# Two-layer attention kernel on TensorE: the order of scores and value blocks in each slot, and what fills the first pass

## Chip, cores and metric

One core of one Trainium2 chip. The metric is the device time of one execution in microseconds (us); runs are compared by their medians.

## What is computed

Two transformer layers on 1024 tokens of 256 features, in float32. The change touches the two 16-head attentions (head size 16): layer 0 reads 4096 given keys and values, layer 1 the 1024 tokens themselves.

```
mod = (_silu(c) @ wmod).reshape(c.shape[0], 6, 1, -1)      # sa, ca, ga, sb, cb, gb, for both layers
h = _layernorm(x, axis=-1) * (1 + ca) + sa
scores = jnp.einsum('bqhd,khd->bhqk', Q, K) * SCALE
attn = jax.nn.softmax(scores, axis=-1)
out = jnp.einsum('bhqk,khd->bqhd', attn, V).reshape(B, QL, HIDDEN)
x = x + ga * (out @ Wo.T)
```

A routed feed-forward follows the first attention, and the normalisation, a causal 16-head attention with 128 features per head and an expert layer follow the second; none of these is edited.

## The kernel before

Class `Attention` runs both attentions; `nkt` is the number of 128-key tiles (32 in the first, called long here; 8 in the second, called short). The work is cut into 32 units: one head and one half (512) of the queries, `u` in the code. The softmax needs the maximum of every query first, so the scores are made twice.

The **first pass** makes scores with queries as output rows. One chunk is 128 queries by 1024 keys: two matmuls (`first_half`, L646) into two of the PSUM banks 0 to 3, one for each strip of the array's rows (rows 0 to 47 hold one part of the keys, rows 64 to 111 the other). VectorE reduces the chunk to its maxima (L786 long, L782 short) and so frees the two banks; two chunks fit at a time. GpSimd splits the maxima into three bf16 parts (`split_max`, L572 to L578), TensorE turns them (`turn_maxima`, L668, L673), and ScalarE writes the row of queries with their maxima (`put_row`, L835).

The **second pass** makes scores with keys as output rows: one matmul for 128 keys (`second_chunk`, L705), on the strip of even or of odd `j`, into one of the banks 4 to 6. ScalarE takes the exponential (L878). Four exponentials make a group, and the **values** of a group (`pv_half`, L686) are four float32 matmuls, side by side in four 32-column parts of the array, into bank 7; a half has 256 query columns, and each float32 matmul appears as two passes in the trace. When a unit's last group is done, the sums in bank 7 are copied out by ScalarE in the long attention (L843) and by VectorE in the short one (L800), and the next unit's first values wait for that copy (`o_full`).

TensorE's order is written by hand in `slot(u, g)`: four second-pass chunks, two first-pass chunks that run `ahead` of them (22 chunks in the long attention, 10 in the short one), and two value halves of the group before. A unit has eight slots in the long attention and two in the short one. Ahead of the first slot, a loop makes the chunks that run ahead. In the long attention it also makes the adaLN modulation (`Front.later_products`): column products (L1051, output 128x1) and row products (L1058, output 128x256). `keep_busy` (L1133) issues bf16 matmuls of 128x128 whose result nobody reads. In the short attention the products of the values (L1246) stand between the first chunks.

Of the kernel before, what the change touches and what calls it, by code (L numbers as in the profile page):

```python
# [18 lines left out]
DC = D // P  # L19
H = 16  # L20
HD = 16
QH = 512
# [294 lines left out]
class Attention:  # L317


    def __init__(self, nc, ctx, psum, ident, ident_bf, tag, nkt, nb, o_dram, k_dram=None, v_dram=None, v_sb=None):  # L320
# [14 lines left out]
        self.pair_last = self.groups >= 8  # L335
        self.sums_by_act = self.groups >= 8
# [63 lines left out]
    def filling(self, j):  # L400
        return j + (j >= self.turn_at)
# [73 lines left out]
    def run(self, block, load_q, load_kr, q_loads, merge, projection, stats, front=None, weights=None):  # L475
# [5 lines left out]
        ahead = steps + self.shift  # L481
# [75 lines left out]
        def _(pool):  # L557
# [71 lines left out]
        def _(pe):  # L629
# [46 lines left out]
            def pv_half(u, n, half):  # L676

                b, cols = (u // 2) % nb, slice(half * (QH // 2), (half + 1) * (QH // 2))
                pe.wait_ge(self.exp_done, u * nkt + group * (n + 1))
                if n == 0 and half == 0:  # L680
                    if u > 0:
                        pe.wait_ge(self.o_full, u)
                    pe.wait_ge(self.v_ready, u // 2 + 1)
                for j in range(group * n, group * (n + 1)):
                    g, block_at = j % 4, (j % 2) * (nkt // 2) + j // 2
                    mm = pe.matmul(psum[32 * g:32 * g + 32, 7, cols], self.v_ext[:, b, block_at, :], self.probs[:, j % self.pring, cols],  # L686
                                   start=(j < 4 and half == 0), stop=(j >= nkt - 4 and half == 1))
                if half == 1:
                    mm.then_inc(self.pv_done, 1)

            def values_behind(u, g, half):

                if g > 0:
                    pv_half(u, g - 1, half)
                elif u > 0:
                    pv_half(u - 1, groups - 1, half)
# [11 lines left out]
            def second_pair(two):  # L708
                if two < self.chunks:
                    first_wait(two)  # L710
                    first_half(two, 0)
                    first_half(two, 1).then_inc(self.s1_full, 1)

            def slot(u, g):

                j = group * g
                one = u * steps + 2 * g + ahead
                two = one + 1
                steps_here = self.steps_after(u, g)
                second_wait(u, j)  # L720
                second_chunk(u, j)
                if one < self.chunks:
                    first_wait(one)
                    first_half(one, 1)
                    first_half(one, 0).then_inc(self.s1_full, 1)
                second_wait(u, j + 1)
                second_chunk(u, j + 1)
                values_behind(u, g, 0)
                if not self.pair_last:
                    second_pair(two)  # L730
# [6 lines left out]
                second_wait(u, j + 3)  # L737
                second_chunk(u, j + 3)
                if self.pair_last:
                    second_pair(two)  # L740
                values_behind(u, g, 1)
# [9 lines left out]
            for n in range(ahead):  # L751
                first_wait(n)
                first_half(n, 0)
                first_half(n, 1).then_inc(self.s1_full, 1)
                if n + values_ahead < projection.tiles:
                    projection.value_products(pe, n + values_ahead)
                if front is not None:
                    front.later_products(pe, n)
            projection.banks_free(pe)
            if front is not None:  # L760
                front.banks_free(pe)
            keep_busy(pe, psum, self.ident_bf, 8)
            turn_maxima(0)
            keep_busy(pe, psum, self.ident_bf, 8)
            for u in range(us):
                for g in range(groups):
                    slot(u, g)
            for half in range(2):
                pv_half(us - 1, groups - 1, half)
# [5 lines left out]
        def _(dve):  # L775
# [31 lines left out]
            for u in range(us):  # L807
                for s in range(steps):
                    if s == 2 and u > 0 and not self.sums_by_act:
# [12 lines left out]
            if not self.sums_by_act:  # L822
                take_sums(us - 1)
# [7 lines left out]
        def _(act):  # L831
# [36 lines left out]
            for u in range(us):  # L868
                for j in range(nkt):
# [3 lines left out]
                    if j == group and u > 0 and self.sums_by_act:  # L873
                        take_sums(u - 1)
# [5 lines left out]
            if self.sums_by_act:  # L880
                take_sums(us - 1)
# [6 lines left out]
class Front:  # L888
# [10 lines left out]
    def __init__(self, room, psum, space, ident, ident_bf, mod_col, mod_row, gates, x, h_t, wq):  # L899
# [27 lines left out]
        groups = [("col", i, c) for i in range(2, len(self.COLS)) for c in range(DC)] + [("row", i, 0) for i in range(len(self.ROWS))]  # L927
        self.groups = sorted(groups, key=lambda g: (self.COLS if g[0] == "col" else self.ROWS)[g[1]][0])
        self.first_chunk = 2

# [134 lines left out]
    def later_products(self, pe, n):  # L1065


        at = n - self.first_chunk
        if not 0 <= at < len(self.groups):
            return  # L1070
        kind, i, c = self.groups[at]
        if at == 0:
            pe.wait_ge(self.wide_ready, 2 * DC)
# [6 lines left out]
    def stay_busy(self, pe):  # L1080


        keep_busy(pe, self.psum, self.ones_bf, 75, 3)
# [1445 lines left out]
```

## Time and profile before

| | before |
|---|---|
| median of 3 runs | 1801.67 us (1797.59 to 1803.48) |
| profiled execution, own time | 1802.71 us |
| profiled execution, span of its instructions | 1800.9 us |
| TensorE, busy share of the span | 96% |
| VectorE | 77% |
| ScalarE | 64% |
| GpSimd | 29% |
| TensorE's mean granted clock, of full speed | 0.976 |

The long attention lies between about 27 and 747 us of the span, the short one between about 804 and 1047 us. Busy shares are averages over stages with different limits, and a busy TensorE at half its clock does half the work; so the stage, its clock and its waits have to be read together.

### The profile page before, as it was taken

Reading aid. Unit: us, or ns where it says so; the run is one execution under the profiler, and the core shown is the slowest. Engines: PE = TensorE matmul, PEld = TensorE weight load, DVE = VectorE, ACT = ScalarE, POOL = GpSimd, SP = SyncE. Lnnn points to the kernel's source line nnn. Section 1 sums busy time; section 2 is a strip of 40 time slices with the busy share of each in tenths; the row PEclk is TensorE's granted clock in tenths of the full one; section 3 lists DMA queues with packets and bytes.
Section 4 is the critical chain, followed back from the end, with each engine's and each line's share of the span. In section 5 each row is a group of like instructions: output and inputs, shape, how many; then the busy total and the mean of one; then the engine's idle time right before and its main releaser. Section 6 shows DMA issues by size and latency. Waiting matters only on the chain. (4 is left out here: it accounts for less than half of the span.)

```text
span 1800.9 us, 34561 instructions
## 1 busy us (share of the span) xinstructions
PE 1720.8 (96%) x13014; PEld 1057.5 (59%) x13017; DVE 1392.3 (77%) x1927; ACT 1147.9 (64%) x2277; POOL 518.5 (29%) x535
## 2 busy tenths in 40 slices
PE   9999999999999999889999989999999999889998
PEld 6433333333333333564444468888888888768886
DVE  5699999999999997367999667777777777746665
ACT  2488888888888888554777635455545554533333
POOL 7247334333344522011334311111211120142221
PEclk8699999999999999989999999999999999989999
DMA  7122232223322300103537210000000000033332
GB/s 174 24 45 59 55 54 50 45 52 70 78 46 57 70 26 11 36 18 61 129 92 167 74 32 16 9 23 15 23 9 23 15 12 1 19 84 109 115 102 77
DMA packets 50309, 97.94 MB, mean 54 GB/s; under 512 B 11481, under 2 KB 21817, under 8 KB 48651
## 3 DMA queue, kind: packets, MB, share of 16 engines
q1 hardware_dynamic: 49899, 95.78, 22.5%
q8 instruction: 82, 1.34, 0.3%
q10 hardware_dynamic: 288, 0.49, 0.2%
q14 instruction: 40, 0.33, 0.1%
HBM read 64.58 MB, written 15.92 MB: 45 GB/s over the span
## 5 line engine op out<-in xcount | busy, mean ns | idle before, releaser
L878 ACT ACTIVATE a_probs<-psum 128x512 f32<-128x512 f32 x1280 | 690.4, 598 | 111.5 <-PE psum L705 81.9
L786 DVE TENSOR_REDUCE a_max_part<-psum 128x1 f32<-128x1024 f32 x512 | 622.0, 1223 | 50.6 <-PE psum L646 48.8
L686 PE MATMUL psum<-a_probs,a_v_ext 128*32 128x256 f32 x5120 | 411.7, 393 | 14.8 <-ACT a_probs L878 7.5
L705 PE MATMUL psum<-a_q_max,a_k_rows 51*128 51x512 f32 x1280 | 399.5, 469 | 0.4 <-ACT a_q_max L835 0.2
L646 PE MATMUL psum<-a_k_rows,a_q_rows 48*128 48x512 f32 x1280 | 367.8, 441 | 4.7 <-DVE a_max_part L786 3.0
L705 PEld LDWEIGHTS psum<-a_q_max,a_k_rows 51*128 51x128 f32 x1280 | 162.4, 185 | 236.7 <-ACT a_probs L878 181.8
L686 PEld LDWEIGHTS psum<-a_probs,a_v_ext 128*32 128x32 f32 x5120 | 103.1, 108 | 238.6 <-ACT a_probs L878 200.5
L646 PEld LDWEIGHTS psum<-a_k_rows,a_q_rows 48*128 48x128 f32 x1280 | 154.9, 189 | 39.1 <-issue 26.2
L782 DVE TENSOR_REDUCE a_neg_max<-psum 128x1 f32<-128x1024 f32 x128 | 153.3, 1222 | 11.0 <-PE psum L646 10.9
L2182 PE MATMUL psum<-high_t_parts,high_gu 128*128 128x512 f32 x600 | 149.0, 398 | 9.1 <-POOL high_gu L2300 7.6
L429 POOL TENSOR_TENSOR a_k_rows<-a_k_in,a_k_rows 16x2048 fp32r<-16x2048 f32 x32 | 146.0, 4562 | 2.5
L572 POOL TENSOR_TENSOR a_max_bf<-a_neg_max,a_zeros 128x8 bf16<-128x8 f32 x64 | 14.7, 229 | 456.0 <-issue 396.5
L2182 PEld LDWEIGHTS psum<-high_t_parts,high_gu 128*128 128x128 f32 x600 | 114.0, 191 | 36.6 <-POOL high_gu L2300 8.2
L1746 PE MATMUL psum<-wide_k_t,wide_q_t 128*128 128x512 f32 (+3 forms) x576 | 130.6, 353 | 1.5 <-DVE wide_k_t L1944 1.5
L1746 PE MATMUL psum<-wide_p_t,wide_v 128*128 128x512 f32 (+3 forms) x576 | 109.5, 343 | 5.1 <-DVE x L1955 5.1
L1746 PEld LDWEIGHTS psum<-wide_p_t,wide_v 128*128 128x128 f32 x576 | 97.6, 188 | 22.3 <-issue 6.3
L1887 ACT ACTIVATE wide_probs<-psum,wide_neg_max 128x128 f32<-128x128 f32 (+7 forms) x128 | 96.5, 754 | 21.6 <-DVE wide_neg_max L1977 21.6
L1966 DVE TENSOR_TENSOR wide_p_t<-psum,wide_p_t 128x512 fp32r<-128x512 f32 (+1 forms) x192 | 100.0, 548 | 12.4 <-ACT wide_p_t L1872 12.4
L1746 PE MATMUL psum<-wide_t_parts,wide_wqk 128*128 128x512 f32 x384 | 102.2, 401 | 6.1 <-DVE wide_v L1944 3.9
L1872 ACT ACTIVATE wide_p_t<-psum 128x512 fp32r<-128x512 f32 (+1 forms) x192 | 87.1, 492 | 28.0 <-PE psum L1787 27.9
L1746 PEld LDWEIGHTS psum<-wide_k_t,wide_q_t 128*128 128x128 f32 x576 | 94.0, 189 | 12.6 <-issue 1.9
L1977 DVE TENSOR_REDUCE wide_neg_max<-psum 128x1 f32<-128x128 f32 (+7 forms) x128 | 97.0, 758 | 4.4
(263 smaller groups left out, 2146.3 us busy)
## 6 DMA issues: line engine op xcount, KB each, us to landing
o<-a_o_out SPq DMA_DIRECT2D x56, 256.0 KB, 2.2
a_k_in<-in_k SPq DMA_DIRECT2D x96, 128.0 KB, 4.5
a_q_rows<-q_high SPq DMA_DIRECT2D x124, 64.0 KB, 2.4
gu_in<-in_w_gu SPq DMA_DIRECT2D x25, 256.0 KB, 2.8
high_cw<-cw SPq DMA_DIRECT2D x22, 256.0 KB, 4.0
a_v_in<-in_v SPq DMA_DIRECT2D x16, 256.0 KB, 5.8
a_o<-o SPq DMA_DIRECT2D x8, 512.0 KB, 4.8
wide_qk_in<-in_wqk SPq DMA_DIRECT2D x16, 256.0 KB, 2.7
```

Of the source, the lines that this page charges most:

```text
L429: pool.tensor_tensor(self.k_rows[low, b, :], self.k_in[low, :], self.k_rows[low, b, :], ALU.subtract).then_inc(self.k_split, 1)
L646: return pe.matmul(psum[:, 2 * (n % 2) + s, :], q_rows[rows, b, q0:q0 + P], k_rows[rows, b, k0:k0 + 512], start=True, stop=True)
L686: mm = pe.matmul(psum[32 * g:32 * g + 32, 7, cols], self.v_ext[:, b, block_at, :], self.probs[:, j % self.pring, cols], start=(j < 4 and h ...
L705: pe.matmul(psum[:, self.bank_of(self.filling(j)), :], k_rows[rows, b, k0:k0 + P], self.q_max[rows, u % 2, :], start=True, stop=True).then ...
L782: dve.tensor_reduce(self.neg_max[:, u % 2, c:c + 1], psum[:, 2 * (n % 2):2 * (n % 2) + 2, :], AX.XY, ALU.max, negate=True).then_inc(self.s ...
L786: dve.tensor_reduce(self.max_part[:, u % 2, c // self.nch, c % self.nch:c % self.nch + 1], psum[:, 2 * (n % 2):2 * (n % 2) + 2, :], AX.XY, ...
L878: act.activation(self.probs[:, p % self.pring, :], psum[:, self.bank_of(self.filling(j)), :], ACT.Exp).then_inc(self.exp_done, 1)
L1746: mm = pe.matmul(out, left(a), right(b), start=(first and n == 0), stop=(last and n == len(PARTS) - 1))
L1887: act.activation(probs[:, i % 2, 0:(i + 1) * P], bank_pair(i)[:, 0:(i + 1) * P], ACT.Exp, bias=neg_max[:, i:i + 1], accum_out=den[:, h % 2 ...
L1966: dve.tensor_tensor(turned_of(i, bank, 1), turned_from(i, bank), turned_of(i, bank, 0), ALU.subtract).then_inc(pt_lo, 1)
L1977: dve.tensor_reduce(neg_max[:, i:i + 1], bank_pair(i)[:, 0:(i + 1) * P], AX.X, ALU.max, negate=True).then_inc(max_ready, 1)
L2182: mm = pe.matmul(psum[:, 2 * (k % 2) + i, :], gu[:, par, a, at:at + P], t_parts[:, b, c, half * 512:(half + 1) * 512], start=(c == 0 and n ...
```

## The change

Four edits. (1) The modulation products are ordered anew: two row products stand ahead of the first chunk, the rest alternate, and `keep_busy` matmuls fill the wait between chunks: three ahead of a chunk with a column product, none ahead of one with a row product, six ahead of one with none. `turn_maxima(0)` moves from behind the loop into it, behind chunk `steps + 2`, with the wait for the free banks; on GpSimd `split_max(0)` moves ahead of the second `copy_v`. (2) In the short attention (`slot_short`) the second first-pass chunk moves up, and the two value halves become one block of 512 columns at the slot's end. (3) The unit without values behind it (`u = 0`, `g = 0`) gets `keep_busy` in their place. (4) In the long attention's second slot (`g == 1`) the third score stands ahead of the first value half.

```diff
                 for h in range(1, self.early):
                     self.split_keys(pool, h)
+                split_max(0)
+                for h in range(1, self.early):
                     self.copy_v(pool, h)
-                split_max(0)
...
+            def values_whole(u, n):
+                values_wait(u, n)
+                values_part(u, n, slice(0, QH), True, True)
...
+            def slot_long(u, g):
+
+                j, ready = group * g, u * steps + 2 * g + ahead
+                behind = (u, g - 1) if g > 0 else (u - 1, groups - 1)
+                steps_here = self.steps_after(u, g)
+                second(u, j)
+                first_pair(ready, (1, 0))
+                second(u, j + 1)
+                if g == 1:
+                    second(u, j + 2)
+                if behind[0] >= 0:
+                    values_half(*behind, 0)
+                else:
+                    keep_busy(pe, psum, self.ident_bf, 8)
+                if g != 1:
+                    second(u, j + 2)
...
+                second(u, j + 3)
+                first_pair(ready + 1, (0, 1))
+                if behind[0] >= 0:
+                    values_half(*behind, 1)
...
+            def slot_short(u, g):
...
+                second(u, j)
+                first_pair(ready, (1, 0))
+                second(u, j + 1)
                 if j + 2 == self.turn_at and u + 1 < us:
                     turn_maxima(u + 1)
+                first_pair(ready + 1, (0, 1))
                 second_wait(u, j + 2)
                 second_chunk(u, j + 2)
...
+                second(u, j + 3)
+                if behind[0] >= 0:
+                    values_whole(*behind)
+                else:
+                    keep_busy(pe, psum, self.ident_bf, 16)
...
             projection.products(pe, front)
             if front is not None:
-                front.stay_busy(pe)
+                projection.banks_free(pe)
+                front.first_products(pe)
...
             for n in range(ahead):
+                t = n + values_ahead
                 first_wait(n)
+                if n >= 2:
+                    filling = front.filling(n) if front is not None else 0 if t < projection.tiles else 6
+                    keep_busy(pe, psum, self.ident_bf, filling, 2 * (n % 2))
                 first_half(n, 0)
...
+                if n == steps + 2:
+                    if front is not None:
+                        front.banks_free(pe)
+                    else:
+                        projection.banks_free(pe)
+                    turn_maxima(0)
...
+        self.groups = [("row", 0, 0), ("row", 1, 0), ("col", 2, 0), ("col", 2, 1), ("col", 3, 0), ("row", 2, 0), ("col", 3, 1),
+                       ("row", 3, 0), ("col", 4, 0), ("row", 4, 0), ("col", 4, 1), ("row", 5, 0), ("col", 5, 0), ("col", 5, 1)]
...
-        keep_busy(pe, self.psum, self.ones_bf, 75, 3)
+    def first_products(self, pe):
+
+
+        keep_busy(pe, self.psum, self.ones_bf, 45, 3)
+        pe.wait_ge(self.wide_ready, 2 * DC)
+        for at in range(self.at_once):
+            self.group_product(pe, at)
```

TensorE's rows at the start of the long attention's first pass, before (`a_c_wide` with `a_o` is a row product, `a_c_silu` a column product; in the changed file the same statements have other line numbers: L1182 is `keep_busy`, L1089 and L1096 the products, L710 `second_chunk`, L689 the values):

```order
L1236 MATMUL psum<-h_t,wq 128x512 x8
L1133 MATMUL psum<-a_ones_bf 128x128 x75
L646 MATMUL psum<-a_k_rows,a_q_rows 128x512 x6
L1051 MATMUL psum<-a_c_silu,a_o 128x1 x2
L646 MATMUL psum<-a_k_rows,a_q_rows 128x512 x2
```

and now:

```order
L1285 MATMUL psum<-h_t,wq 128x512 x8
L1182 MATMUL psum<-a_ones_bf 128x128 x45
L1096 MATMUL psum<-a_o,a_c_wide 128x256 x4
L646 MATMUL psum<-a_k_rows,a_q_rows 128x512 x4
L1182 MATMUL psum<-ident_bf 128x128 x3
L646 MATMUL psum<-a_k_rows,a_q_rows 128x512 x2
L1089 MATMUL psum<-a_c_silu,a_o 128x1 x2
```

Two row products have come ahead of chunk 0, and three fillings ahead of chunk 2.

The long attention's second slot on TensorE, before (`a0_o_full` is the copy of the sums):

```order
L705 MATMUL psum<-a_q_max,a_k_rows 128x512 [waits a0_exp_done]
L646 MATMUL psum<-a_k_rows,a_q_rows 128x512 [waits a0_s1_free]
L646 MATMUL psum<-a_k_rows,a_q_rows 128x512
L705 MATMUL psum<-a_q_max,a_k_rows 128x512 [waits a0_exp_done]
L686 MATMUL psum<-a_probs,a_v_ext 32x256 [waits a0_v_ready,a0_o_full,a0_exp_done]
L686 MATMUL psum<-a_probs,a_v_ext 32x256 x3
L705 MATMUL psum<-a_q_max,a_k_rows 128x512 [waits a0_exp_done] x2
```

and now:

```order
L710 MATMUL psum<-a_q_max,a_k_rows 128x512 [waits a0_exp_done]
L646 MATMUL psum<-a_k_rows,a_q_rows 128x512 [waits a0_s1_free]
L646 MATMUL psum<-a_k_rows,a_q_rows 128x512
L710 MATMUL psum<-a_q_max,a_k_rows 128x512 [waits a0_exp_done] x2
L689 MATMUL psum<-a_probs,a_v_ext 32x256 [waits a0_v_ready,a0_o_full,a0_exp_done]
L689 MATMUL psum<-a_probs,a_v_ext 32x256 x3
L710 MATMUL psum<-a_q_max,a_k_rows 128x512 [waits a0_exp_done]
L646 MATMUL psum<-a_k_rows,a_q_rows 128x512 [waits a0_s1_free]
```

One score has moved from behind the value half that waits for `a0_o_full` to ahead of it, and the score that stood beside it stays behind.

A unit of the short attention on TensorE, before, from its turned maxima to the next unit:

```order
L668 MATMUL psum<-a_q_rows,a_ident_r 115x512
L673 MATMUL psum<-ident_bf,a_max_bf 115x128 x4
L705 MATMUL psum<-a_q_max,a_k_rows 128x512 x2
L686 MATMUL psum<-a_probs,a_v_ext 32x256 x4
L705 MATMUL psum<-a_q_max,a_k_rows 128x512
L646 MATMUL psum<-a_k_rows,a_q_rows 128x512 x2
L705 MATMUL psum<-a_q_max,a_k_rows 128x512
L686 MATMUL psum<-a_probs,a_v_ext 32x256 x4
L646 MATMUL psum<-a_k_rows,a_q_rows 128x512 x2
L705 MATMUL psum<-a_q_max,a_k_rows 128x512 x2
```

and now:

```order
L668 MATMUL psum<-a_q_rows,a_ident_r 115x512 [waits a1_exp_done]
L673 MATMUL psum<-ident_bf,a_max_bf 115x128 [waits a1_max_ready]
L673 MATMUL psum<-ident_bf,a_max_bf 115x128 x3
L646 MATMUL psum<-a_k_rows,a_q_rows 128x512 [waits a1_s1_free]
L646 MATMUL psum<-a_k_rows,a_q_rows 128x512
L710 MATMUL psum<-a_q_max,a_k_rows 128x512 [waits a1_exp_done] x2
L689 MATMUL psum<-a_probs,a_v_ext 32x512 [waits a1_exp_done]
L689 MATMUL psum<-a_probs,a_v_ext 32x512 x3
L710 MATMUL psum<-a_q_max,a_k_rows 128x512 [waits a1_row_ready]
L646 MATMUL psum<-a_k_rows,a_q_rows 128x512 [waits a1_q_loaded3,a1_s1_free]
```

Four value halves of a unit have become two blocks, each at the end of its slot, and the first-pass chunk that stood behind the turned maxima's half now follows the turned maxima.

## Rows read from the trace of the kernel before

**Rows 1.** Windows: us, busy of TensorE, its weight loads, VectorE, ScalarE, GpSimd; granted clock; DMA.
```profile
30.40:40.60 10.20, 10.20 (x30) 6.37 (x30) 6.98 (x6) 0.00 (x0) 5.87 (x2) 0.50 0.81 129
...
86.60:107.30 20.70, 20.45 (x201) 7.81 (x197) 19.56 (x17) 18.29 (x35) 12.54 (x7) 1.00 0.37 64
```

**Rows 2.** Timeline of TensorE, first pass and first slots, long attention: start, us, group [idle before].
```profile
23.02 4.35 PE L1133 MATMUL psum<-a_ones_bf 128*128 128x128 bf16 x75
29.14 0.51 PE L646 MATMUL psum<-a_k_rows,a_q_rows 48*128 48x512 f32 x2 [1.09 <-DVE a_max_part L786]
...
35.93 2.07 PE L1058 MATMUL psum<-a_o,a_c_wide 128*128 128x256 f32 x4
...
41.63 0.50 PE L646 MATMUL psum<-a_k_rows,a_q_rows 48*128 48x512 f32 x2
...
42.60 0.49 PE L646 MATMUL psum<-a_k_rows,a_q_rows 48*128 48x512 f32 x2
...
64.90 0.79 PE L705 MATMUL psum<-a_q_max,a_k_rows 51*128 51x512 f32 x1
...
79.47 0.50 PE L705 MATMUL psum<-a_q_max,a_k_rows 51*128 51x512 f32 x1
...
81.93 0.49 PE L705 MATMUL psum<-a_q_max,a_k_rows 51*128 51x512 f32 x1
```

**Rows 3.** Timeline of VectorE and GpSimd, the same stretch.
```profile
23.70 1.29 DVE L1283 SCALAR_TENSOR_TENSOR q_low<-psum,q_high 128x512 fp32r<-128x512 f32 x2 [2.59 <-ACT q_high L1268]
27.86 4.62 DVE L786 TENSOR_REDUCE a_max_part<-psum 128x1 f32<-128x1024 f32 x4 [2.88 <-PE psum L646]
38.33 9.09 POOL L429 TENSOR_TENSOR a_k_rows<-a_k_in,a_k_rows 16x2048 fp32r<-16x2048 f32 x2
```

**Rows 4.** Timeline of TensorE, value products between chunks, short attention.
```profile
821.98 1.13 PE L1246 MATMUL psum<-wqkv,h_t 128*128 128x256 f32 x4
```

**Rows 5.** Timeline of TensorE and ScalarE, a second slot of the long attention.
```profile
113.10 0.73 PE L646 MATMUL psum<-a_k_rows,a_q_rows 48*128 48x512 f32 x2
114.08 0.64 PE L686 MATMUL psum<-a_probs,a_v_ext 128*32 128x256 f32 x8 [0.25 <-issue]
113.38 0.60 ACT L843 ACTIVATE a_o_out<-psum 128x512 f32<-128x512 f32 x1
```

**Rows 6.** TensorE's waits, 78 to 706 us: us in total, times, longest.
```profile
PE psum L686 <- issue: 7.2, 29, 0.2
```

**Rows 7.** Timeline of TensorE, one unit of the short attention.
```profile
847.83 0.51 PE L646 MATMUL psum<-a_k_rows,a_q_rows 48*128 48x512 f32 x2
848.26 0.49 PE L668 MATMUL psum<-a_q_rows,a_ident_r 112*115 112x512 f32 x1
...
849.34 0.64 PE L686 MATMUL psum<-a_probs,a_v_ext 128*32 128x256 f32 x8
849.91 0.49 PE L705 MATMUL psum<-a_q_max,a_k_rows 51*128 51x512 f32 x1
...
850.84 0.64 PE L686 MATMUL psum<-a_probs,a_v_ext 128*32 128x256 f32 x8 [0.19 <-ACT a_probs L878]
...
854.31 0.48 PE L668 MATMUL psum<-a_q_rows,a_ident_r 112*115 112x512 f32 x1
```

**Rows 8.** Timeline of VectorE and ScalarE, the same unit; below, the copy's group in the page's manner.
```profile
847.35 2.36 DVE L782 TENSOR_REDUCE a_neg_max<-psum 128x1 f32<-128x1024 f32 x2 [0.22 <-PE psum L646]
846.12 2.08 ACT L878 ACTIVATE a_probs<-psum 128x512 f32<-128x512 f32 x4 [0.60 <-PE psum L705]
L800 DVE COPY a_o_out<-psum 128x512 f32<-128x512 f32 x32 | 22.1, 691 | 10.2 <-PE psum L686 10.2
```

**Rows 9.** Timeline of TensorE, short attention: its first second-pass scores and one of its last units.
```profile
835.09 0.79 PE L705 MATMUL psum<-a_q_max,a_k_rows 51*128 51x512 f32 x1
...
842.21 0.49 PE L668 MATMUL psum<-a_q_rows,a_ident_r 112*115 112x512 f32 x1
...
1023.32 0.64 PE L686 MATMUL psum<-a_probs,a_v_ext 128*32 128x256 f32 x8 [0.99 <-ACT a_probs L878]
```

More of the change, by code:

```diff
@@ L334, in __init__ @@
         self.early = 2
-        self.pair_last = self.groups >= 8
-        self.sums_by_act = self.groups >= 8
+        self.long = self.groups >= 8
         self.room = room = Room(nc, ctx, tag, CLEARED)
@@ L683, in pv_half, with values_part @@
                     pe.wait_ge(self.v_ready, u // 2 + 1)
+            def values_part(u, n, cols, first, last):
+                b = (u // 2) % nb
                 for j in range(group * n, group * (n + 1)):
@@ L686, in pv_half, with values_half @@
                     mm = pe.matmul(psum[32 * g:32 * g + 32, 7, cols], self.v_ext[:, b, block_at, :], self.probs[:, j % self.pring, cols],
-                                   start=(j < 4 and half == 0), stop=(j >= nkt - 4 and half == 1))
-                if half == 1:
+                                   start=(j < 4 and first), stop=(j >= nkt - 4 and last))
+                if last:
                     mm.then_inc(self.pv_done, 1)
[L691 to L696, printed above, removed]
+            def values_whole(u, n):
+                values_wait(u, n)
+                values_part(u, n, slice(0, QH), True, True)
+            def values_half(u, n, half):
+                if half == 0:
+                    values_wait(u, n)
+                values_part(u, n, slice(half * (QH // 2), (half + 1) * (QH // 2)), half == 0, half == 1)
             def second_wait(u, j):
@@ L706, in second_chunk, with first_pair @@
                           self.q_max[rows, u % 2, :], start=True, stop=True).then_inc(self.s2_full, 1)
[L708 to L719, printed above, removed]
+            def first_pair(n, order):
+                if n < self.chunks:
+                    first_wait(n)
+                    first_half(n, order[0])
+                    first_half(n, order[1]).then_inc(self.s1_full, 1)
@@ L720, in slot, with second @@
+            def second(u, j):
+                if j == self.turn_at and u + 1 < us:
+                    turn_maxima(u + 1)
                 second_wait(u, j)
                 second_chunk(u, j)
[L722 to L730, printed above, removed]
+            def slot_long(u, g):
[13 more added lines that the diff above has]
+                    second(u, j + 2)
+                for k in steps_here[:1]:
+                    merge.product(pe, k)
+                second(u, j + 3)
[3 more added lines that the diff above has]
+                else:
+                    keep_busy(pe, psum, self.ident_bf, 8)
+                for k in steps_here[1:]:
+                    merge.product(pe, k)
@@ L731, in slot @@
+            def slot_short(u, g):
+                j, ready = group * g, u * steps + 2 * g + ahead
+                behind = (u, g - 1) if g > 0 else (u - 1, groups - 1)
+                steps_here = self.steps_after(u, g)
+                second(u, j)
+                first_pair(ready, (1, 0))
+                second(u, j + 1)
                 if j + 2 == self.turn_at and u + 1 < us:
                     turn_maxima(u + 1)
+                first_pair(ready + 1, (0, 1))
                 second_wait(u, j + 2)
@@ L751, in _ @@
             for n in range(ahead):
+                t = n + values_ahead
                 first_wait(n)
+                if n >= 2:
+                    filling = front.filling(n) if front is not None else 0 if t < projection.tiles else 6
+                    keep_busy(pe, psum, self.ident_bf, filling, 2 * (n % 2))
                 first_half(n, 0)
                 first_half(n, 1).then_inc(self.s1_full, 1)
-                if n + values_ahead < projection.tiles:
-                    projection.value_products(pe, n + values_ahead)
+                if t < projection.tiles:
+                    projection.value_products(pe, t)
                 if front is not None:
                     front.later_products(pe, n)
[L759 to L764, printed above, removed]
+                if n == steps + 2:
+                    if front is not None:
+                        front.banks_free(pe)
+                    else:
+                        projection.banks_free(pe)
+                    turn_maxima(0)
             for u in range(us):
                 for g in range(groups):
-                    slot(u, g)
-            for half in range(2):
-                pv_half(us - 1, groups - 1, half)
+                    if self.long:
+                        slot_long(u, g)
+                    else:
+                        slot_short(u, g)
+            values_whole(us - 1, groups - 1)
             for k in range(in_slots, merge.STEPS):
@@ L808, in _ @@
                 for s in range(steps):
-                    if s == 2 and u > 0 and not self.sums_by_act:
+                    if s == 2 and u > 0 and not self.long:
                         take_sums(u - 1)
@@ L821, in _ @@
                     merge.reciprocals(dve, 1)
-            if not self.sums_by_act:
+            if not self.long:
                 take_sums(us - 1)
@@ L872, in _ @@
                         put_row(u + 1)
-                    if j == group and u > 0 and self.sums_by_act:
+                    if j == group and u > 0 and self.long:
                         take_sums(u - 1)
@@ L1078, in later_products, with filling @@
             mm.then_inc(self.later_full, 1)
-    def stay_busy(self, pe):
-        keep_busy(pe, self.psum, self.ones_bf, 75, 3)
+    def first_products(self, pe):
[3 more added lines that the diff above has]
+            self.group_product(pe, at)
+    def later_products(self, pe, n):
+        at = n - self.first_chunk + self.at_once
+        if n >= self.first_chunk and at < len(self.groups):
+            self.group_product(pe, at)
+    def filling(self, n):
+        at = n - self.first_chunk + self.at_once
+        if at >= len(self.groups):
+            return 6
+        return 3 if self.groups[at][0] == "col" else 0
     def banks_free(self, pe):
```

22 lines of the change are left out of this document (5 added, 17 removed).

## The prediction

> **What bounds the kernel now.** I read the page's clock and busy rows first, then windows of each stage, then the timeline of TensorE there, then what its waits end on. A steady slot of the long attention is TensorE's: in 86.6 to 107.3 us it is busy 20.45 of 20.70 us at full clock, with VectorE close behind at 19.56 [rows 1]. The slot lasts 2.46 (79.47 to 81.93) [rows 2]. A value half holds the array 0.57 (849.34 to 849.91, the same instructions in the short attention) [rows 7], so the four score steps of a slot take (2.46 - 2 x 0.57) / 4 = 0.33 each. Two places are worse than that. In the long attention's first pass TensorE is busy all of 30.4 to 40.6, yet at a granted clock of 0.50, the lower of its two levels, 1.2 GHz [rows 1]; the first four slots, 64.90 to 79.47, take 14.57 instead of 9.84 [rows 2]. And a unit of the short attention takes 6.05 (848.26 to 854.31) [rows 7], where its work, below, is shorter.
>
> **Edit 1 and 3, the long front.** The fillings now stand behind q_low, whose two operations end at 23.70 + 1.29 = 24.99 [rows 3]. A filling is 4.35 / 75 = 0.058 [rows 2], so 45 end at 27.6. No row shows a row product at full clock; half of the 2.07 that one took at the lower clock is 1.03 [rows 2], and four passes of the same size took 1.13 at full [rows 4]. I take 1.06. Two put chunk 0 at 29.72, and VectorE's first reduction, half a microsecond behind its pair, at 30.26: 2.4 later than the 27.86 of before [rows 3]. From there VectorE's pace is 4.62 / 4 = 1.155 [rows 3], and chunk 2 waits for the first reduction's end, 31.42. A chunk with a column product takes TensorE 0.97 at full clock (41.63 to 42.60) [rows 2], with three fillings 1.14: VectorE's pace stands. A chunk with a row product takes 0.43 (a pair, 847.83 to 848.26 [rows 7]) + 1.06 = 1.49. Chunks 2 to 13 have eight of the one and four of the other, 8 x 1.155 + 4 x 1.49 = 15.2, to 46.6. Seven paces on, chunk 21 starts at 54.7; with its pair, and 0.3 for the part of the turned maxima that VectorE's lead doesn't cover, the first score stands at 55.4 instead of 64.90 [rows 2]. That is **-9.5**, if the clock stays at full.
>
> The fillings of the last chunks hide in VectorE's pace: six are 0.35, beside 0.43 of a pair. The moved turn hangs on GpSimd, whose key split ends at 38.33 + 9.09 = 47.42 [rows 3]; chunk 15, the last that unit 0 needs, is reduced about 49 to 50, so the key split ends first, and with `split_max(0)` ahead of the second `copy_v` the turn finds its maxima about when TensorE gets there. If it waited for `copy_v` again, that would be about 1 us. The first four slots at full clock, one with 16 x 0.058 of fillings in place of its values, are 2.2 + 3 x 2.46 = 9.6 instead of 14.57: **-5.0**. Bounds for both: 0, and -16 if the turn costs nothing. What is late next is VectorE, which then paces the front alone.
>
> The clock is the open term. Before, it fell behind a stretch whose longest idle was 1.09 us [rows 2], rose by itself, and fell once more behind pairs and column products without a wait (from 41.63 [rows 2] on; at 64.90 a score takes 0.79, at 79.47 0.50). Now chunks 2 to 4 are again pairs and column products, with three fillings each, but 45 fillings and two row products stand ahead, and row products alternate behind. In the Trainium skill, TensorE: Matmul & The Clock Gate, the section on why this matters for your kernels puts a lost clock down to long idle gaps between bursts. By that rule the front would not have fallen before; the trace has it fall behind 1.09 us and behind no idle, so the measurement decides, and the rule alone would give the 14.5 for certain.
>
> **Edit 4, the long second slot.** The first value half waits there for ScalarE's copy of the sums (113.38 + 0.60 = 113.98) and starts at 114.08 [rows 5]; the trace counts 29 such waits, 7.2 us together, 0.25 each [rows 6]. A slot has two score steps ahead of the half, 0.66, and the half starts 0.98 behind the slot (113.10 to 114.08) [rows 5]: 0.32 are lost, the slot is 2.78. Now the third score fills that wait. But scores run two abreast, one on each strip, and this one stood beside the fourth on the other strip. Alone it holds the array a step of 0.33, and the fourth one then pairs with half a first-pass chunk and leaves the other half alone: five steps in place of four, 2.46 + 0.33 = 2.79. The wait goes and the time stays: 31 x 0.01, **+0.3**; ends -8 (both wait and step gone: 31 x 0.25) and +3 (a step 0.1 dearer). I take the middle because the steps on one strip are counted, not guessed. The Trainium skill, TensorE: Matmul & The Clock Gate, Part 3 (the mechanism), says that a weight load passes a running matmul only if the row groups differ; for a score alone on its strip that would make the step dearer, towards the +3, and no run here shows it.
>
> **Edit 2, the short loop.** A pass of 256 columns alone takes 1.13 / 4 = 0.28 [rows 4], some 2 x 0.107 (256 columns at 2.4 GHz) and a rest. A half block's eight passes take 0.57, so its four column parts run abreast: two passes one behind the other, 2 x 0.21 = 0.43 that grows with the columns, and 0.14 that I take not to. A whole block is then 0.86 + 0.14 = 1.00, against 1.14 for two halves: 2 x 0.14 a unit. The other bound is 1.14, nothing saved. The wait of 0.19 at 850.84 [rows 7] goes, since the block stands at the slot's end. Two pairs that stood alone at 0.43 [rows 7] stand beside scores at 0.33 now: 0.2. So TensorE's work falls from 6.05 to 5.38. VectorE's own is four reductions of 2.36 / 2 = 1.18, less their overlap 1.15, and a copy of 0.69: 5.3 [rows 8]. A new wait: ScalarE needs 2.08 / 4 = 0.52 an exponential [rows 8], scores now stand close together ahead of the block, and the last of a group waits for a bank: some 0.15. I take 5.5, a gain of 0.55; ends 0.28 (only the columns' part) and 0.75 (down to VectorE). Behind 842.21 there are 28 units at this pace: 28 x 0.55 = **-15.4** (-8 to -21). What is late next is VectorE. The front of this attention: from 835.09 to 842.21 the first unit takes 7.12 [rows 9], 1.07 over the loop's pace, because it starts behind fillings and at the lower clock; a full-clock start and the earlier turn give **-2.4** (0 to -4). In the tail two waits of 1.0 (one at 1023.32 [rows 9], one alike 8.6 later) lose their cause: **-2.0** (0 to -2).
>
> **The sum.** -9.5 - 5.0 + 0.3 - 15.4 - 2.4 - 2.0 = -34.0, made against the profiled execution of 1802.71 us: 1768.7. The median is 1.0 under that execution, so I forecast **1768**.
>
> **Rivals.** *The clock falls again in chunks 2 to 5* (34%). For it: pairs and column products stood there when it fell before. Against: the fillings. At the lower clock the slots took 14.57 / 9.84 = 1.48 times as long; 1.48 to 2 times the 15.2 of chunks 2 to 13 is 7 to 15 more, and the first score stands at 63 to 70 against 64.90. The front then gives nothing, -3 to +5: 1782, 1778 to 1788. *The short loop stays at its pace* (8%): a new wait takes the whole 0.55, for instance the turn behind `put_row`, or ScalarE. 1783; with the clock's fall as well (5%) 1797. *Slower: a 512-column value block does not run abreast as the halves do* (6%). Eight passes at 0.28 would be 2.2 where a half takes 0.57, so the halves run abreast; but no row shows a block of 512. Two abreast, its eight passes of 0.43 to 0.53 would take 1.7 to 2.1. From 1.28 on the loop gains nothing; from 1.71 on (28 x 2 x 0.43 = 24) it eats the front's 19 and 5 more, and at 1.8 to 2.1 the kernel takes 1812 to 1829. *The change does less than it says*: edit 4 does, by my own count; it is in the sum.
>
> **How the numbers follow.** The forecast has 47%: 1768, its own ends 1762 and 1778. The clock's fall and the unchanged short loop stand at 1782 and 1783. The range 1762 to 1788 takes these in and leaves out the two together, the slower case, and what lies under 1762. A measurement of this kernel can tell about 0.3%, 5.4 us, from no change. Under 1796: 47 + 34 + 8 = 89%. Within: 5%. Over: 6%.
>
> **What would show it.** Right: a granted clock of 1.00 from 30 to 60 us, the first score near 55, slots of 2.46 from there; no wait at the first value half of second slots, but slots of 2.79 still; units of 5.5 in the short attention with a block near 1.0. Wrong: a score of 0.79 in the first slots (clock), a second slot near 2.5 (edit 4 priced too low), a value block over 1.28, or a new wait of 0.5 on `a_exp_done` or `a_row_ready` in each short unit.

## The result, and the profile after

Twenty executions of the changed kernel have a median of 1796.46 us (1775.25 to 1810.96), twenty of the kernel before 1801.21. The ratio is 0.9939, with an interval of 0.9913 to 0.9964: by the ratio about 11 us faster, where 1768 was forecast and 1762 to 1788 was the range. The ratios, here and below, leave out executions more than 1.5% above the fastest of their kernel, here eight of the changed kernel, seven of them with the lowest clocks, and one of before; the two medians over all twenty lie only 4.7 apart.

The twenty don't lie around their median. Three are at 1775 to 1781, nine at 1791 to 1798, one at 1802, seven at 1808 to 1811, and TensorE's mean granted clock goes with them: 0.984 to 0.989 in the first three, 0.971 to 0.977 in the nine, 0.963 to 0.967 in the seven. The profiled execution is one of the long ones, 1808.55, span 1806.7, clock 0.965. Windows of its long attention (us; busy of TensorE, weight loads, VectorE, ScalarE, GpSimd; clock; DMA) show where:

```profile
24.50:32.70 8.20, 7.11 (x73) 5.49 (x73) 3.28 (x3) 0.59 (x2) 5.09 (x3) 1.00 0.65 101
32.90:68.70 35.80, 35.80 (x150) 23.17 (x150) 22.05 (x20) 2.50 (x9) 14.79 (x8) 0.50 0.37 62
68.90:118.00 49.10, 49.10 (x271) 17.91 (x268) 27.67 (x24) 25.18 (x46) 14.79 (x8) 0.50 0.13 25
118.20:138.90 20.70, 20.70 (x201) 7.98 (x197) 19.15 (x18) 17.74 (x34) 0.89 (x4) 1.00 0.14 31
```

One stretch at the lower clock reaches from 32.8 to 118.1, over the first pass and some eleven slots behind it (a unit has eight), TensorE busy throughout. Before, two stretches at the lower clock ended at 40.6 and 78.2. The timeline of TensorE at its start, the first score, and a slot's length at half clock, from behind the first value half of one slot to the same place in the next:

```profile
28.88 0.73 PE L646 MATMUL psum<-a_k_rows,a_q_rows 48*128 48x512 f32 x4
30.70 0.34 PE L1182 MATMUL psum<-ident_bf 128*128 128x128 bf16 x3 [1.09 <-DVE a_max_part L823]
30.97 0.50 PE L646 MATMUL psum<-a_k_rows,a_q_rows 48*128 48x512 f32 x2
31.40 0.60 PE L1089 MATMUL psum<-a_c_silu,a_o 128*128 128x1 f32 x4
...
33.64 0.79 PE L646 MATMUL psum<-a_k_rows,a_q_rows 48*128 48x512 f32 x2
...
68.79 0.62 PE L710 MATMUL psum<-a_q_max,a_k_rows 51*128 51x512 f32 x1
...
75.65 0.79 PE L710 MATMUL psum<-a_q_max,a_k_rows 51*128 51x512 f32 x1
...
79.97 0.79 PE L710 MATMUL psum<-a_q_max,a_k_rows 51*128 51x512 f32 x2
```

The wait of 1.09 for chunk 0's reduction is still there [rows 2], chunks 2 to 4 are pairs and column products with three fillings, and the pair of chunk 4, at 33.64, takes 0.79 instead of 0.50. The first score is at 68.79 (64.90 before), the last score of the long attention at 763.29 (743.06): 20.2 lost where 14.2 gained was forecast. Of that, 3.9 is the first pass and 16.3 the slots. A slot at half clock takes 4.32 (75.65 to 79.97), one at full clock 2.46 [rows 2]: 1.76 times as long, not twice. Behind the first score, 49 us ran at half clock where before 13.3 did; the 36 more cost 36 x (1 - 1/1.76) = 15.5 by these rows, an estimate, which is nearly all of the 16.3.

In the second slots the 29 waits [rows 6] are gone: the waits of TensorE between 120 and 725 us are empty. A unit still takes 20.64 us (20.65 before). A unit of the short attention takes 5.70 instead of 6.05 [rows 7]. TensorE in one, then ScalarE and a weight load of TensorE (PEld):

```profile
873.13 0.50 PE L710 MATMUL psum<-a_q_max,a_k_rows 51*128 51x512 f32 x1
...
873.93 0.88 PE L710 MATMUL psum<-a_q_max,a_k_rows 51*128 51x512 f32 x2
874.74 1.06 PE L689 MATMUL psum<-a_probs,a_v_ext 128*32 128x512 f32 x8
875.73 0.49 PE L710 MATMUL psum<-a_q_max,a_k_rows 51*128 51x512 f32 x1
...
876.40 0.49 PE L668 MATMUL psum<-a_q_rows,a_ident_r 112*115 112x512 f32 x1
...
877.84 1.06 PE L689 MATMUL psum<-a_probs,a_v_ext 128*32 128x512 f32 x8
878.83 0.49 PE L710 MATMUL psum<-a_q_max,a_k_rows 51*128 51x512 f32 x1
```

```profile
873.66 2.06 ACT L915 ACTIVATE a_probs<-psum 128x512 f32<-128x512 f32 x4 [0.46 <-PE psum L710]
874.31 0.18 PEld L710 LDWEIGHTS psum<-a_q_max,a_k_rows 51*128 51x128 f32 x1 [0.42 <-ACT a_probs L915]
```

A block holds the array 0.99 (874.74 to 875.73). The third and fourth score of a second slot stand 0.81 ahead of it, where a step of two is 0.33: that is a new wait, 0.42 of the fourth's weight load (874.31) for an exponential. From the first short chunk to the first score the two traces give 15.03 and 13.30, from there to the turn of unit 29 170.54 and 160.48, from there to the last score 27.90 and 26.66. The short attention gained 1.73 + 10.06 + 1.24 = 13.0, of 19.8 forecast.

### The profile page after: what moved, and what is told of

The parts are those of the page before. It is cut to its first block and busy times, and to the rows that moved or that the text cites. A ratio compares the mean times of both kernels' runs of the same rounds, so it can differ in the third digit from the quotient of the medians.

```text
span 1806.7 us, 33654 instructions
## 1 busy us (share of the span) xinstructions
PE 1742.8 (96%) x12560; PEld 1066.0 (59%) x12563; DVE 1391.1 (77%) x1927; ACT 1147.2 (63%) x2277; POOL 518.5 (29%) x535
## 5 line engine op out<-in xcount | busy, mean ns | idle before, releaser
L710 PE MATMUL psum<-a_q_max,a_k_rows 51*128 51x512 f32 x1280 | 424.8, 472 | 0.8 <-ACT a_probs L915 0.7
L689 PE MATMUL psum<-a_probs,a_v_ext 128*32 128x256 f32 (+1 forms) x4600 | 403.9, 423 | 0.4
L646 PE MATMUL psum<-a_k_rows,a_q_rows 48*128 48x512 f32 x1280 | 377.4, 446 | 0.0
L710 PEld LDWEIGHTS psum<-a_q_max,a_k_rows 51*128 51x128 f32 x1280 | 175.9, 188 | 281.8 <-ACT a_probs L915 223.2
L689 PEld LDWEIGHTS psum<-a_probs,a_v_ext 128*32 128x32 f32 x4600 | 92.1, 109 | 203.2 <-issue 133.7
L646 PEld LDWEIGHTS psum<-a_k_rows,a_q_rows 48*128 48x128 f32 x1280 | 160.8, 193 | 10.1 <-issue 5.1
```

Source lines behind the costliest of these rows:

```text
L646: return pe.matmul(psum[:, 2 * (n % 2) + s, :], q_rows[rows, b, q0:q0 + P], k_rows[rows, b, k0:k0 + 512], start=True, stop=True)
L710: pe.matmul(psum[:, self.bank_of(self.filling(j)), :], k_rows[rows, b, k0:k0 + P], self.q_max[rows, u % 2, :], start=True, stop=True).then ...
```

## Which part loses the clock

**The old first pass under the other edits.** The long attention's first pass is put back, and with it the place of `split_max` on GpSimd and the long first slot without fillings (edit 3); the short attention and the long second slot stay changed.

```diff
-                projection.banks_free(pe)
-                front.first_products(pe)
+                front.stay_busy(pe)
...
-                    filling = front.filling(n) if front is not None else 0 if t < projection.tiles else 6
+                    filling = 0 if front is not None or t < projection.tiles else 6
...
+            if front is not None:
+                projection.banks_free(pe)
+                front.banks_free(pe)
+                keep_busy(pe, psum, self.ident_bf, 8)
+                turn_maxima(0)
+                keep_busy(pe, psum, self.ident_bf, 8)
```

> The changed kernel with the long attention's first pass as it was before (75 fillings, products in the old order, no fillings between chunks, the turn behind the loop); the short attention and the long second slot stay changed. Theory F (the new first pass loses TensorE's clock, and the short attention's gain of 13.0, read from the two traces as 1.7 + 10.75 + 0.55, stands in every run): 13 us under before, ratio 0.9928 within 0.0015, and the executions lie as close together as those of before; the clock is back at 1.00 by about 80 us. Rival S (the lone third score of the long second slot keeps the clock down, whatever the first pass does): the executions still scatter by 30 us and the clock comes back later than 100 us in most of them; the ratio is 0.994 or more.

Measured: 1788.90 (1782.78 to 1803.99, 11 executions) against 1805.12, ratio 0.9904 (0.9874 to 0.9935). The 13 us of theory F, 0.9928, lie inside. So undoing the new first pass makes the kernel no slower; whether it makes it faster isn't shown, since the interval overlaps that of the change (0.9913 to 0.9964). Its other half was wrong: the clock is not back by 80 in every execution. In the profiled one, at 1803.99, it came back for 6.6 us and fell again:

```profile
31.20:51.50 20.30, 20.30 (x60) 12.84 (x58) 12.90 (x11) 0.00 (x0) 13.88 (x4) 0.50 0.54 89
51.70:58.30 6.60, 4.71 (x20) 2.37 (x20) 5.79 (x6) 1.90 (x8) 0.90 (x4) 1.00 0.39 60
58.50:123.20 64.70, 64.20 (x350) 24.05 (x350) 37.38 (x34) 31.99 (x59) 15.70 (x12) 0.50 0.13 21
```

**The third score alone**, added to the kernel before.

```diff
+                early = self.pair_last and g == 1
+                if early:
+                    third(u, j + 2)
                 values_behind(u, g, 0)
```

> The kernel before with one edit alone: in the long attention's second slot the third score stands ahead of the first value half. Theory F: no difference, ratio 1.000 within 0.002; a unit of the long attention stays at 20.64 to 20.66 us, the 29 waits of 0.25 are gone. Rival S: the clock stays at half past 100 us in many executions, 5 to 20 us slower. A third reading (the step on one strip costs nothing after all): 7 us faster, a unit of 20.4.

Measured: 1806.34 (12 executions, 1800.11 to 1840.53), ratio 1.0031 (0.9998 to 1.0065), just outside the 0.002 of theory F. No gain: a unit is 20.64, and the waits are gone. Mean clocks were 0.971 over these twelve and 0.975 over the 22 of before; whether the move delays the clock's return by a little is left open.

**The first pass filled.** The row products stand behind chunks 0 and 1, where they cover the wait of 1.09, and thin chunks (a pair with a column product or with nothing behind it) get more fillings.

```diff
-        self.first_chunk = 2
-        self.at_once = 2
+        self.first_chunk = 0
+        self.at_once = 0
...
-            return 6
-        return 3 if self.groups[at][0] == "col" else 0
+            return 8
+        if self.groups[at][0] == "row":
+            return 0
+        return 10 if n in (2, 3, 4, 12, 13) else 3
```

> The changed kernel, but the two row products stand behind chunks 0 and 1 instead of ahead of chunk 0, where they cover TensorE's wait for chunk 0's reduction, and there are ten fillings instead of three ahead of chunks 2, 3, 4, 12 and 13, eight instead of six ahead of 14 to 21. Theory F: the granted clock is 1.00 from 24 us into the slots, the first score stands near 55, the first slots take 2.46; all executions lie between 1770 and 1780, ratio 0.984 within 0.003. If the idle time and the thin products are not what loses the clock: it falls as in the changed kernel, with executions from 1775 to 1810, ratio 0.99 or more.

Measured: 1776.03, all six executions between 1773.92 and 1779.10, mean clock 0.988 to 0.991, ratio 0.9854 (0.9819 to 0.9889). Its windows:

```profile
24.50:32.70 8.20, 6.88 (x72) 5.37 (x72) 3.89 (x5) 1.91 (x3) 4.48 (x3) 1.00 0.86 124
32.90:57.90 25.00, 23.96 (x201) 16.83 (x202) 22.05 (x20) 2.50 (x9) 14.82 (x8) 1.00 0.48 85
58.00:68.20 10.20, 10.20 (x98) 4.40 (x95) 10.06 (x10) 8.23 (x16) 0.00 (x0) 1.00 0.01 2
```

The clock holds in the profiled execution. The first score stands at 57.97, with chunk 0 at 28.43, so it comes 3 later than the 55 expected. The ratio's interval lies below 1 and below that of the change.

**Each half of that alone.** First, only the two row products behind chunks 0 and 1, with the change's own three and six fillings:

```diff
-        self.first_chunk = 2
-        self.at_once = 2
+        self.first_chunk = 0
+        self.at_once = 0
```

> Of the filled front one half alone: the two row products stand behind chunks 0 and 1 (they cover TensorE's wait for chunk 0's reduction), the fillings are the changed kernel's three and six. If the idle 1.09 us is what loses the clock: it holds, executions between 1770 and 1778, a shade under the filled front since five chunks carry seven fillings less, 0.4 each. If the thin products (a pair and a column product a chunk) lose it: it falls between 31 and 36 us and the executions scatter from 1775 to 1810.

Measured: 1781.70 over six executions, against 1796.49 for before at that time. Three lie at 1770 to 1774 (clock 0.991), three at 1790, 1800 and 1806. The profiled one fell:

```profile
24.50:33.80 9.30, 9.22 (x77) 6.70 (x75) 6.09 (x6) 0.00 (x0) 3.63 (x3) 1.00 0.65 113
34.00:85.00 51.00, 51.00 (x243) 27.82 (x241) 30.86 (x27) 12.29 (x27) 14.77 (x8) 0.50 0.19 37
```

TensorE was busy 9.22 of the 9.30 us ahead of the fall. So the clock fell behind three chunks with column products (from 29.6 on) with next to nothing idle. The rule of the Trainium skill that the prediction weighed (TensorE: Matmul & The Clock Gate, why this matters for your kernels), by which long idle gaps lose the clock, doesn't cover this fall. Second, only the fillings, with the row products ahead of chunk 0 and the wait in place:

```diff
-        return 3 if self.groups[at][0] == "col" else 0
+        return 10 if n in (2, 3, 4, 12, 13) else 3
```

> The other half alone: ten fillings ahead of chunks 2, 3, 4, 12 and 13 and eight ahead of 14 to 21, but the two row products ahead of chunk 0 as in the changed kernel, so that the wait of 1.09 us stays. If the idle time loses the clock: it falls near 33 us, executions from 1780 to 1810. If the thin products do: it holds, executions between 1774 and 1781.

Measured: 1776.77 over seven executions, ratio 0.9898 (0.9863 to 0.9934): five at 1772 to 1779, two at 1784 and 1790 with clocks of 0.985 and 0.982. In the profiled one the wait of 1.09 ends at 29.91 and the clock held at 1.00:

```profile
28.09 0.73 PE L646 MATMUL psum<-a_k_rows,a_q_rows 48*128 48x512 f32 x4
29.91 0.73 PE L1184 MATMUL psum<-ident_bf 128*128 128x128 bf16 x10 [1.09 <-DVE a_max_part L823]
...
56.56 0.39 PE L710 MATMUL psum<-a_q_max,a_k_rows 51*128 51x512 f32 x1
```

So neither half alone is the whole cause: by the mean clock each by itself lets most or half of the executions hold, where the change held in two of twenty at 0.988 or more. The small counts don't rank the halves. What remains open is why one execution of a kernel keeps the clock and the next doesn't, and whether the fillings hold it by their own work or by spacing the column products out: no run has a pause of the same length in their place.

**Fewer fillings**, seven for ten and six for eight.

```diff
-        return 10 if n in (2, 3, 4, 12, 13) else 3
+        return 7 if n in (2, 3, 4, 12, 13) else 3
```

> The filled front with seven fillings in place of ten ahead of chunks 2, 3, 4, 12 and 13, and six in place of eight ahead of 14 to 21. If what fills the thin products decides: between three fillings (the clock fell in half the executions) and ten (in none of six): it holds in most of them, those at 1771 to 1775, 1 us under the filled front; a fall shows as 1780 to 1805.

Measured: 1774.36, against 1803.73 for before at that time, five of six at 1771 to 1775 and one at 1801 (clock 0.972). In the profiled one the clock held and the first score stood at 55.15, behind a chunk 0 that came early:

```profile
26.89 0.50 PE L646 MATMUL psum<-a_k_rows,a_q_rows 48*128 48x512 f32 x2 [0.53 <-POOL a_k_rows L428]
...
55.15 0.39 PE L710 MATMUL psum<-a_q_max,a_k_rows 51*128 51x512 f32 x1
```

One fall in six against none in six doesn't tell the two numbers of fillings apart, and a microsecond less is within the spread of the executions.

## What the long second slot and the short loop are worth

**The filled first pass without the third score's move**, so that the clock doesn't blur the comparison.

```diff
                 second(u, j + 1)
-                if g == 1:
-                    second(u, j + 2)
...
-                if g != 1:
-                    second(u, j + 2)
+                second(u, j + 2)
```

> The filled front and the changed short attention, without the third score's move in the long second slot: the 29 to 31 waits of 0.25 us are back. Theory (the wait goes and a step on one strip comes): within 2 us of the filled front with the move (1776.0), a unit of 20.64 to 20.69 in both. Rival (the move is worth the wait that it removes): 7 us slower than with it, a unit of 20.9.

Measured: 1775.84 over six executions, against 1776.03 with the move; units of 20.65 and 20.68. The two were run at different times (before's medians were 1796.49 and 1805.12), so the slots in the traces decide more than the 0.2 between the medians. A second slot without it, then one with it, on TensorE:

```profile
142.80 0.49 PE L710 MATMUL psum<-a_q_max,a_k_rows 51*128 51x512 f32 x1
...
143.78 0.64 PE L689 MATMUL psum<-a_probs,a_v_ext 128*32 128x256 f32 x8 [0.25 <-issue]
...
145.58 0.49 PE L710 MATMUL psum<-a_q_max,a_k_rows 51*128 51x512 f32 x1
```

```profile
143.26 0.49 PE L710 MATMUL psum<-a_q_max,a_k_rows 51*128 51x512 f32 x1
...
143.61 0.62 PE L710 MATMUL psum<-a_q_max,a_k_rows 51*128 51x512 f32 x2
144.25 0.64 PE L689 MATMUL psum<-a_probs,a_v_ext 128*32 128x256 f32 x8
...
146.04 0.49 PE L710 MATMUL psum<-a_q_max,a_k_rows 51*128 51x512 f32 x1
```

Both slots last 2.78. The wait is exchanged for a step, as counted. The score alone on its strip and the step ahead of it take 0.64 together (143.61 to 144.25), so the dearer step that the prediction drew from the Trainium skill (TensorE: Matmul & The Clock Gate, Part 3, the mechanism) isn't there. Two of the six had a clock of 0.984 and 0.986, so the filled first pass doesn't hold it every time either.

**The value block as two halves**, one behind the other.

```diff
-                    values_whole(*behind)
+                    values_half(*behind, 0)
+                    values_half(*behind, 1)
```

> The changed kernel with the value block of 512 columns in the short attention put back into two halves of 256 columns, one right behind the other, at the same place. Read from its profile: a unit of the short attention, 5.70 us in the changed kernel. Theory: the 0.14 of each block that does not grow with its columns comes back twice a unit: 5.98. Rival: the waits for ScalarE's exponentials set the pace and hide it: 5.70 to 5.80.

Measured in its profile (time 1799.59): a unit of 5.71, not 5.98.

```profile
874.23 1.07 PE L689 MATMUL psum<-a_probs,a_v_ext 128*32 128x256 f32 x16
875.23 0.49 PE L710 MATMUL psum<-a_q_max,a_k_rows 51*128 51x512 f32 x1
```

The number agrees with the rival, but not for its reason: the halves themselves take 1.00, as the whole block does, and nothing had to hide them. By these durations the 0.14 that doesn't grow with the columns belongs to each stay of the array with the values, whether one block or two halves stand in it, and not to each instruction. The saving was two such stays a unit instead of four; the merged instruction gives nothing.

**Half an exponential.** In the short attention, from the third unit on, the fifth score's exponential covers 256 of its 512 columns and leaves older values in the rest.

```diff
+                    cols = slice(0, QH // 2) if j == 4 and u >= 2 and not self.long else slice(0, QH)
```

> The filled front, and in the short attention from the third unit on ScalarE takes the exponential of the fifth score (the first of a unit's second slot) over 256 of the 512 columns; the other columns keep older values. Theory (the slot's length is the chain from the fifth score over its exponential to the eighth score, which takes the same bank, and then the value block): the unit falls from 5.70 by what the exponential gets shorter, 0.2 to 0.27, to 5.43 to 5.50. Rival (VectorE's four reductions and copy, or TensorE's own work, set the pace): 5.60 to 5.70.

Measured in its profile: units of 5.49. TensorE, then ScalarE and the eighth score's weight load:

```profile
874.71 0.50 PE L710 MATMUL psum<-a_q_max,a_k_rows 51*128 51x512 f32 x1
...
875.52 0.66 PE L710 MATMUL psum<-a_q_max,a_k_rows 51*128 51x512 f32 x2
876.11 1.07 PE L689 MATMUL psum<-a_probs,a_v_ext 128*32 128x512 f32 x8
```

```profile
875.25 1.85 ACT L916 ACTIVATE a_probs<-psum 128x256 f32<-128x256 f32 x4 [0.46 <-PE psum L710]
875.68 0.18 PEld L710 LDWEIGHTS psum<-a_q_max,a_k_rows 51*128 51x128 f32 x1 [0.21 <-ACT a_probs L916]
```

The two last scores now take 0.59 to the block instead of 0.81, and the unit is shorter by 0.21, as much as ScalarE's four (1.85 against 2.06). The weight load waits 0.21 where it waited 0.42. The wait on the fifth exponential is shown.

**The fifth score early**, ahead of the first slot's block, to take that wait away.

```diff
+                if g == 0:
+                    second(u, j + 4)
+                    if ready + 2 < self.chunks:
+                        first_wait(ready + 2)
+                        first_half(ready + 2, 1)
                 if behind[0] >= 0:
                     values_whole(*behind)
```

> The filled front, and in the short attention the fifth score of a unit stands ahead of the first slot's value block, abreast with the first half of the next first-pass chunk; the sixth score and the chunk's other half open the second slot. No step is added. Theory (the chain from the fifth score over its exponential to the eighth is what the second slot's length was): its 0.28 us of waiting goes, a unit of 5.40 to 5.45 instead of 5.70, 7 us under the filled front: 1767 to 1771, ratio 0.985 within 0.004. Rival (VectorE at 5.3 and the block that the fifth exponential must now wait for): 5.6 or more, 1773 or more.

Measured: 1783.52, ratio 0.9877 (0.9830 to 0.9923), units of 5.86 and 5.92: a miss. Rows of TensorE's weight loads and of ScalarE, a second slot first (861.04, 861.69), then the first slot behind it:

```profile
861.04 2.06 ACT L925 ACTIVATE a_probs<-psum 128x512 f32<-128x512 f32 x4 [0.62 <-PE psum L689]
861.69 0.18 PEld L710 LDWEIGHTS psum<-a_q_max,a_k_rows 51*128 51x128 f32 x1 [0.32 <-ACT a_probs L925]
...
864.53 0.42 PEld L710 LDWEIGHTS psum<-a_q_max,a_k_rows 51*128 51x128 f32 x2
865.27 0.18 PEld L710 LDWEIGHTS psum<-a_q_max,a_k_rows 51*128 51x128 f32 x1 [0.31 <-ACT a_q_max L882]
```

```profile
864.61 0.60 ACT L882 ACTIVATE a_q_max<-psum 115x512 fp32r<-115x512 f32 x1
```

The second slot fell to 2.27 from 2.60, but only by the step of 0.33 that moved out of it. Its wait is still there: the fifth exponential starts at 861.04, when the value block is done, as the rival said, and the eighth score's weight load waits 0.32 for it. And the fifth score takes the bank of the turned maxima, which ScalarE frees only at 865.21, so the first slot waits too: 3.65 instead of 3.10, a step and 0.22 more. The old wait stayed and a new one came.

## Why the prediction was wrong

- **The clock, in the front's sum: failed.** "Against: the fillings" was the step. Three fillings a chunk did not hold the clock over chunks 2 to 4; by the mean clock the change held it in two executions of twenty (0.988 or more), and with more fillings (ten for three, eight for six) and nothing else changed five of seven lay at 1772 to 1779. The rival that named this fall had 34%, and its 1782 (1778 to 1788) was too low as well.
- **The rival's price: failed, and this makes the median.** It set the front at -3 to +5 and let the slots end as before. In the profiled execution the long attention lost 20.2, most of it because the clock came back at 118.1 and not at 78.2, over slots in which TensorE was always busy. Over the profiles in which it fell it came back at 78, 79, 85, 88, 118 and 123 us. So the time of return has to be priced as a spread of some 45 us, and one trace of before doesn't show it. The pace was read wrong too: 1.48 comes from four slots of which the first had no values and the last ended at full clock; a slot at half clock takes 1.76 times as long. By that, 45 us are worth 19 (an estimate), about the distance from 1791 to 1811.
- **The front with a held clock: about right, as far as a variant shows it.** No execution of the change itself with a held clock was profiled. From chunk 0 to the first score the forecast was 25.7 (29.72 to 55.4); with ten fillings it took 28.5 (28.09 to 56.56), and the 51 fillings more are up to 3.0 at 0.058 each. The 55.15 with seven fillings is partly luck, since chunk 0 came at 26.89. The first four slots and the second slots held their terms: from the first to the last long score the same variant took 673.5 for 678.2, 4.6 less, where 4.7 was forecast. The filled first pass, at 1776.0, lies 12.9 under the 1788.9 of the old one with the same other edits, where 14.5 was forecast.
- **The long second slot: right.** 2.79 forecast, 2.78 measured, the wait gone and no time with it.
- **The short loop: the place of the new wait right, its size and one reason wrong.** 5.5 forecast, 5.70 measured, a gain of 0.35 for 0.55, and 13.0 over the short attention for 19.8: this alone puts the forecast 6.8 too low, whatever the clock did before, and 1768 + 6.8 = 1775 is about where the fastest of the twenty lies. The block was right at 1.00 by luck: two halves one behind the other take 1.00 as well, so the merge isn't what saved it. The new wait was set at 0.15 and lay on the right place: fifth score, its exponential, eighth score; it is 0.28 (a second slot of 2.60 where four steps and a block are 2.32), and the first slot has another 0.13 over its 2.97 (four steps, the turned maxima's 0.65, a block). The front of the short attention gave 1.73 for 2.4, the tail 1.24 for 2.0, where new waits stand: two of 0.8 on the copy of the sums and one of 0.7 on an exponential.
- **The rival on the slower side: wrong.** Blocks of 512 columns do run as the halves do: 0.99 for one.

## What to carry to other kernels

Before fillings or thin products are priced, ask what clock they will run at, and price the return as well as the fall: in one profile the half clock outlasted the last column product by 62 us (56.1 to 118.1), through slots that ran at full clock later on. Look at many executions, not one profile, when their times lie in groups. A wait that is removed by reordering buys time only if no step is added, and a score moved ahead takes on the waits of its own bank.

## What the runs showed of the hardware

- The clock fell to half behind 9.30 us of which TensorE was busy 9.22, and it held behind a wait of 1.09 where thick fillings stood after it: idle time alone doesn't decide.
- A steady loop with TensorE always busy ran at half clock for 49 us, after which the clock rose by itself; in the profiles of other variants, with nearly the same loop, it rose as early as 78 and 79 us. A slot of it took 4.32 at half clock and 2.46 at full.
- Two value blocks of 256 columns in a row take 1.00, one of 512 takes 0.99, and one of 256 between scores 0.57.
